# Two attention layers on one core: the single jobs of the first layer placed at other steps, and the softmax denominators' short gaps begun twelve units earlier

## What is computed

```python
px = avg_pool_3x3_s2(x)                         # 28 x 28 keys
q = conv1x1(x, w_qs, b_qs); k = conv1x1(px, w_qs, b_qs); v = conv1x1(px, w_vs, b_vs)
pi = softmax(mix_w @ mean(q))                   # weight of each of two parts of 8 channels
out = sum over parts of pi * softmax(q_part @ k_part / 4) @ v
x = conv1x1(out, w_out) * bn_gamma / sqrt(1 + 1e-5) + bn_beta + x
```

```python
xn = (x - mean_c(x)) / sqrt(var_c(x) + 1e-5) * gamma      # over the 128 channels
q, k, v = split(w_qkv @ xn)                                # 8 heads of 16
h = leaky(w0 @ rel + b0); h = leaky(w1 @ h + b1); bias = w2 @ h + b2   # rel: signed log distances
x = x + w_out @ (softmax(q @ k / 4 + bias) @ v)
```

## Time and profile before

| | |
|---|---|
| median of three executions | 3918.48 us (3915.25, 3918.48, 3929.6) |
| the profiled execution: its time | 3944.19 us |
| its span | 3942.2 us |
| TensorE busy in the span | 3749.5 us, 95%, 27690 matmuls |
| VectorE, ScalarE, POOL busy | 2739.9, 2394.8, 848.9 us |
| mean granted TensorE clock | 0.94 of full |
| first layer, units 0 to 55 | 49.4 to 1390.7 us |
| second layer, units 56 to 83 | 1390.7 us to the end |

### The profile page before, as it was taken

The page is one execution under the profiler, slowest core; times in us unless marked ns, Lnnn a source line. Parts: engine busy times, 40 slices in busy tenths (PEclk is TensorE's granted clock), DMA queues, the critical chain, the costliest instruction groups (busy, mean ns, idle before and its releaser), DMA issues.

```text
span 3942.2 us, 70851 instructions
## 1 busy us (share of the span) xinstructions
PE 3749.5 (95%) x27690; PEld 1043.3 (26%) x27690; DVE 2739.9 (70%) x8284; ACT 2394.8 (61%) x2830; POOL 848.9 (22%) x935
## 2 busy tenths in 40 slices
PE   7998899899887999999999999999999999999998
PEld 2222222222222222222222222222222222222221
DVE  5567777777765777766777666777776677777770
ACT  3556766766766256666566666566666656666665
POOL 2143433434525111122101012101112201000000
PEclk6779998989978699999999999999999999999999
DMA  1288888200002023222223222232232222232320
GB/s 51 17 57 56 58 59 55 27 15 19 18 15 72 22 63 92 70 67 70 68 72 82 70 70 70 70 86 74 70 84 79 71 68 70 67 86 74 82 56 26
DMA packets 268053, 236.35 MB, mean 60 GB/s; under 512 B 222184, under 2 KB 225112, under 8 KB 267464
## 3 DMA queue, kind: packets, MB, share of 16 engines
q1 hardware_dynamic: 241544, 205.85, 27.8%
q0 software_dynamic: 26176, 25.98, 3.1%
HBM read 226.65 MB, written 27.19 MB: 64 GB/s over the span
## 4 chain that ended last, share of the span: by engine, by line
PE 80%; DVE 8%; issue 7%; POOL 2%; ACT 2%; DMA 1%; POOLq 0%; SPq 0%; ACTq 0%; DVEq 0%
PE P L731 25%; PE P L716 18%; PE P L684 15%; PE P L697 7%; DVE maxes L1046 7%; PE P L673 5%; PE P L757 4%; PE P L807 2%; PE P L701 2%; PE P L784 1%; POOL high L539 1%; PE P L773 1%; PE P L819 1%; DVE junk L1065 0%; ACT L984 0%
## 5 line engine op out<-in xcount | busy, mean ns | idle before, releaser
L935 ACT ACTIVATE probs<-P 128x896 f32<-128x896 f32 (+1 forms) x2352 | 2117.2, 916 | 1359.2 <-PE P L716 964.2
L1065 DVE CUSTOM_DVE_ANT_0 junk<-P,mstage 112x448 bf16<-112x448 f32 x3136 | 1773.6, 621 | 675.7 <-PE P L684 675.2
L731 PE MATMUL P<-probs,vals 128*17 128x448 f32 (+1 forms) x9408 | 1181.2, 576 | 11.9 <-ACT sums L1011 11.7
L1046 DVE TENSOR_REDUCE maxes<-P 128x1 f32<-128x392 f32 (+1 forms) x1600 | 796.4, 558 | 338.2 <-PE P L673 337.5
L716 PE MATMUL P<-bstage,flip 112*56 112x448 f16 x6272 | 887.1, 363 | 0.0
L684 PE MATMUL P<-keys,q_stack 48*112 48x448 f16 x3136 | 740.2, 400 | 10.6 <-DVE maxes L1065 9.1
L697 PE MATMUL P<-q_two,keys 49*128 49x448 f16 x3136 | 642.2, 352 | 0.0
L684 PEld LDWEIGHTS P<-keys,q_stack 48*112 48x112 f16 x3136 | 284.7, 124 | 887.9 <-DVE maxes L1065 468.0
L673 PE MATMUL P<-keys,q_stack 24*128 24x392 f16 (+1 forms) x1600 | 416.8, 369 | 84.5 <-DVE maxes L1046 52.7
L539 POOL TENSOR_SCALAR high<-projected,cst 128x448 f16<-128x448 f32 x112 | 157.0, 1402 | 1385.0 <-ACT projected L944 1335.2
L716 PEld LDWEIGHTS P<-bstage,flip 112*56 112x56 f16 x6272 | 210.6, 104 | 572.8 <-issue 572.8
(11 more groups left out here) (129 smaller groups left out, 1444.6 us busy)
## 6 DMA issues: line engine op xcount, KB each, us to landing
mstage<-g_max SPq DMA_DIRECT2D x56, 1519.0 KB, 8.0
bstage<-g_bias SPq DMA_DIRECT2D x28, 1568.0 KB, 8.1
bstage<-g_bias SPq DMA_DIRECT2D x28, 1519.0 KB, 7.9
g_max<-t_bf SPq DMA_DIRECT2D x16, 673.8 KB
keys<-d_rden POOLq DMA_DIRECT2D x42, 224.0 KB, 6.0
rwide<-d_rden POOLq DMA_DIRECT2D x42, 224.0 KB, 4.9
g_bias<-t_hi SPq DMA_DIRECT2D x8, 679.9 KB
g_bias<-t_lo SPq DMA_DIRECT2D x8, 679.9 KB
```

The lines of the kernel that those rows point to most:

```text
L731: last = mm(P[32 * h:32 * h + HD + 1, PV, 0:QB], table[0:kr, kt, h, :], probs[0:kr, s % 3, h, :], start=kt == 0, stop=kt == unit.tiles - 1 ...
L935: A(probs[0:kr, s % 3, 2 * p:2 * p + 2, :], P[0:kr, 2 * p:2 * p + 2, 0:QB], ACT.Exp).then_inc(exp_done, 1)
L1046: V.tensor_reduce(out=maxes0[0:size, unit.i % 2, t, HALVES[r], c:c + 1], in_=P[0:size, bank_of(job), 0:HALF], op=ALU.max, axis=AX.X).then_ ...
L1065: V.tensor_tensor_reduce(out=junk[:, PLAN.nth[job] % 4, :], in0=P[0:QT, bank_of(job), 0:QB], in1=bias, scale=1.0, scalar=-3.0e38, op0=ALU. ...
```

## The change

- `SLOW` goes from 42 to 30. With it the gaps of `stages` shrink from unit 24 on instead of 36 and are two steps from unit 28 instead of 40; units 30 to 41 use `sums` and `rwide`; and `keys[0]` is cleared at steps 223 to 230 instead of 307 to 314.
- The 21 network jobs go from steps 0 to 20 (one in each) to steps 2, 3 and 5 of each of units 0 to 6; the last is at step 47.
- The seven pairs `m`, `w` of the first batch go from steps 350 to 363 (units 50 and 51, one job in each step) to the third and fourth step of units 34 to 40, one pair in each unit.
- The 14 key and 4 value jobs of group 8 go from steps 364 to 381 (one in each) to steps 315 to 367, one in about every third step.
- The value job of groups 1 to 7 goes from four steps behind the first key job to nine behind it.
- Group 8's weights are loaded at step 305 and scaled at 312. Groups 6 and 7 still need their biases then, so there are four buffers of biases, chosen by `biases_of`.

No instruction of arithmetic is added or taken away.

```diff
--- before.py
+++ after.py
@@ -49,7 +49,7 @@
 
 
 
-SLOW, SUMS0, RDEN = 42, 6, 4
+SLOW, SUMS0, RDEN = 30, 6, 4
 CLEARS = 7
 GROUPS0, GROUPS1 = 4, 2
 FIRST1 = NB * GROUPS0 * ROWS8
@@ -168,7 +168,7 @@
                 put(BASE[i] - 1, "b", "s", i, 0)
             put(STAGES[i]["projected"], "b", "o", i)
         for n in range(len(NET)):
-            put(n, "b", "n", n)
+            put(7 * (n // 3) + (2, 3, 5)[n % 3], "b", "n", n)
         put(2, "b", "x", 0)
         put(4, "b", "x", 1)
         for group in range(1, len(UNITS) // ROWS8):
@@ -177,9 +177,11 @@
                 at = BASE[first.i - 3]
                 put(at, "b", "k", group, 0, 0)
                 put(at + 2, "b", "k", group, 1, 0)
-                put(at + 4, "b", "v", group, 0)
+                put(at + 9, "b", "v", group, 0)
                 continue
             before = range(BASE[first.i - 4], BASE[first.i - 2] + UNITS[first.i - 2].tiles - 3)
+            if first.i == FIRST1:
+                before = range(BASE[FIRST1 - 11], BASE[FIRST1 - 3])
             todo = [("k", group, n, p) for n in range(7) for p in range(2)] + [("v", group, m) for m in range(4)]
             for k, job in enumerate(todo):
                 put(before[k * len(before) // len(todo)], "b", *job)
@@ -187,7 +189,8 @@
             first = FIRST1 + b * GROUPS1 * ROWS8
             steps = range(BASE[first - 6], BASE[first - 4])
             for n in range(7):
-                at = steps[2 * n * len(steps) // 14]
+
+                at = steps[2 * n * len(steps) // 14] if b else BASE[FIRST1 // NB + 6 + n] + 2
                 put(at, "b", "m", b, n)
                 put(at + 1, "b", "w", b, n)
 
@@ -237,7 +240,7 @@
         bar = sb("bar", [128, BW])
         pi = sb("pi", [128, 8])
         wg = [sb(f"wg{k}", [128, WG]) for k in range(2)]
-        biases = [sb(f"biases{k}", [128, AW]) for k in range(2)]
+        biases = [sb(f"biases{k}", [128, AW]) for k in range(4)]
         quarter = [sb(f"quarter{k}", [128, 3]) for k in range(2)]
         marks = sb("marks", [128, 4])
         keys = [sb(f"keys{k}", [128, 2, 28 * 128], F16) for k in range(2)]
@@ -335,6 +338,9 @@
         q_flat = q_stack[:, :, :].rearrange("k a n -> k (a n)")
         mean = cst[:, C_MEAN:C_MEAN + 128]
         IDLE0 = PLAN.last("qk", lambda j: j[1] < (FIRST1 if j[0] == "q" else NB * GROUPS0))
+
+        def biases_of(group):
+            return group % 2 + 2 * is_biased(group)
 
         def landed(j):
             return 16 * (j // 2 + 1)
@@ -485,6 +491,7 @@
                     blocks = wg[k][:, QW:QW + 512].rearrange("c (s j) -> c s j", j=64)
                     G.tensor_scalar(narrow[k][:, 0, :, 0:24], blocks[:, 0:4, 0:24], 1.0, None, ALU.mult)
                     G.tensor_scalar(narrow[k][:, 1, :, 0:24], blocks[:, 4:8, 0:24], HD ** -0.5, None, ALU.mult)
+                k = biases_of(group)
                 G.tensor_scalar(biases[k][:, A_Q:A_Q + n], qb, 1.0, None, ALU.mult)
                 G.tensor_scalar(biases[k][:, A_K:A_K + n], kb, HD ** -0.5, one, ALU.mult, ALU.add).then_inc(wg_ready, 1)
 
@@ -604,13 +611,16 @@
                 if s == BASE[8]:
                     pool_source(1)
                 for group in range(2, len(UNITS) // ROWS8):
-                    early_load = group < NB * GROUPS0
+                    early_load = group <= NB * GROUPS0
                     at = BASE[(group - 1) * ROWS8] + 4 if early_load else STAGES[(group - 1) * ROWS8 - 1]["projected"] + 1
+                    if group == NB * GROUPS0:
+                        at = BASE[(group - 2) * ROWS8 + 1] + 4
                     if s == at:
                         if early_load:
 
 
-                            pool.wait_ge(copied, PLAN.last("qk", lambda j: group_of(j) == group - 2))
+                            if not is_biased(group):
+                                pool.wait_ge(copied, PLAN.last("qk", lambda j: group_of(j) == group - 2))
                             pool.wait_ge(vals_made, PLAN.last("v", lambda j: j[1] == group - 2))
                             pool.wait_ge(wg_ready, group - 1)
                             pool.wait_ge(wout_ready, group - 1)
@@ -619,7 +629,7 @@
                         load_group(pool, group)
                     if s == at + 7:
                         scale_weights(group)
-                    if early_load and s == BASE[group * ROWS8] + 10:
+                    if not is_biased(group) and s == BASE[group * ROWS8] + 10:
                         weigh_output(group)
 
         @block.tensor
@@ -936,7 +946,7 @@
 
             def take_projection(job):
                 _, p, width = stack_source(job)
-                k, n = group_of(job) % 2, PLAN.nth[job]
+                k, n = biases_of(group_of(job)), PLAN.nth[job]
                 at = (A_Q, A_K)["qk".index(job[0])] + p
                 act.wait_ge(proj_made, n + 1)
                 if n >= 2:
```

## The result

The changed kernel takes 3980.0 us (median of four runs, 3971.4 to 3997.2) against 3922.3 (median of four, 3915.3 to 3929.6): ratio 1.0153, 95% interval 1.0111 to 1.0195. It is slower by 1.5%, with an interval clear of 1, and outside the forecast range of 3889 to 3948. An execution over 1.5% above the fastest of its kernel is left out of every mean, median and ratio here. The profiled execution is the slowest of the four, with a span of 3995.2 us; the one of the kernel before, with 3942.2, was also dearer than that kernel's median, so the two profiles do not stand for the medians in every stretch.

What follows compares the result with a forecast made beforehand. First-layer units were taken as paced by steps of 2.14 us, extra jobs at 1.2 us and TensorE's half clock. Terms 22 + 2 + 6 + 2 - 33 = -1 gave 3919 us against the median, no change; range 3889 to 3948.

Steps and rivals of the forecast that it cites:

- SLOW 30: Units 28 to 33: short denominator transfers stall while the table is spread; loss 33 us, bounds 10 and 50.
- short legs that don't bite: Rival 1: back-to-back denominator transfers land fast or the spread ends before unit 30; loss at most 5, 3891 us, chance 0.26.
- My ring in POOL's order: Units 28 to 33: product, next load, store back, broadcast, product wait on each other; a 29.8 us turn against 20.2 a unit.
- Keys, values and value jobs: Group 8's jobs out of units 52 to 54, gain 6 us; other groups' value jobs five steps later, gain 2.
- The network: Units 0 to 6: jobs over seven units raise TensorE's granted clock to 0.80; gain 22 us, bounds nothing and 40.
- nothing, if the share stays: Lower bound of the network's gain in units 0 to 6: no gain if the granted clock share does not change.
- The moments: Pairs moved to units 34 to 40: 4.0 us a pair stays of 4.4; gain 2 us, bounds -5 and 14.
- seven pauses, each of which may drop the clock: Lower bound of the moments' term over units 34 to 40: -5 us.
- Rival 2: The ring bites and units 0 to 6 keep their clock: loss 45, gains 15, 3948 us; chance 0.24.
- what would show it: Signs named beforehand: times of units 0 to 6, 28 to 33, 34 to 40, 50 to 55, the spread and the second layer.

Runs made afterwards that it cites:

- e1: The whole change but with SLOW 42 as in the kernel before; median 3944.4 us, ratio to the kernel before 1.0077.
- e13: The changed kernel with POOL's load of the next denominators moved ahead of the product of the unit before; median 3978.0 us, ratio to the kernel before 1.0159.
- e7: The kernel before with only the change's keys, values, value jobs and biases, and the moment pairs packed over units 43 and 44; median 3901.1 us, ratio 0.9923.
- e17: The same kernel as e7, run again in another group; median 3903.4 us, ratio to the kernel before 0.9971.
- e8: e7 with the network dealt over units 0 to 6 as in the change; median 3915.4 us, ratio to the kernel before 0.9988.
- e4: The kernel before with only the first batch's moments moved, one pair a unit over units 34 to 40; median 3927.0 us, ratio 1.0036.
- e9: e4 with three extra 128x448 matmuls on constants in the step behind each w job; median 3920.5 us, ratio to the kernel before 0.9996.
- e14: The changed kernel with three extra 128x448 matmuls in the step behind each first-batch w job; median 3970.2 us, ratio to the kernel before 1.0137.
- e12: e7 with the output projection of units 40 to 55 one step earlier and POOL's clearing of keys[0] begun a step later; ratio to the kernel before 1.001.
- e18: The same kernel as e12, run again in another group; ratio to the kernel before 0.9996.
- e2: The whole change, but the seven first-batch moment pairs one job a step over units 39 and 40; median 3974.1 us, ratio to the kernel before 1.0105.
- e10: The kernel before with one extra 64-column matmul in each first-layer step that has a first-pass group; median 4162.6 us, ratio 1.0576.
- e5: The kernel before with SLOW 30 alone; mean span 3950.9 us, ratio 1.0078.
- e15: The same kernel as e5, run again in another group; mean span 3933.5 us, ratio to the kernel before 1.0045.

## Why the prediction was wrong

**SLOW 30: right that short legs stall beside the spread, and close in size.** The step was a loss of 33 with a turn of 29.8 us and a spread that ends 116 us into unit 28. Measured: legs of 24.0 us in sum for 26.0, turns of 28.2, 25.7 and 22.6, a spread that ends near 815 us, 123 us into unit 28, and, by e1 against the change, a loss of 32 to 36. I had 28 for stalls and 5 for POOL and the clock; the split says 22 and 14, and some 7 of the 14 were stalls at the half clock, so the make-up was about right too. Units 29 to 33 of the profiles: 148.4 us at 0.73 against 103.0 at 0.94 is 148.4 x 0.27 x 2/3 = 27 lost to the clock against 4, and 23 of waits. The chance I gave to short legs that don't bite (0.26) is answered by the two rows of waits. My ring in POOL's order, however, is not shown: e13 opened it at one edge and nothing changed.

By the Trainium skill ("DMA: Bandwidth & Descriptors", the part on the two cost components) a turn would have been some 6.5 us plus handovers, an estimate from its fixed and per-byte cost. Beside the spread this trace does not agree: the three legs alone took 24.0 us.

**Keys, values and value jobs: right in sign, the gain larger.** The terms were 6 and 2, and 2 for the moments as packed as before. Before to e7 and e17 gained 25 and 16 us, of which only 5 are waits and work. Units 52 to 54 fell by 20.5 us, to 77 where 70 was forecast, since their jobs went elsewhere; the wait of ScalarE on POOL's stacks, 7.5 us before, is gone, and that on the denominator load, 6.2 us, which I left standing, is 1.1 us. The rest of the gain is clock, which I did not size and which no run explains.

**The network: the first step that failed.** "I take a granted 0.80" for units 0 to 6 rested on the thought that single jobs raise the clock, so more units with jobs have more rises. In the two profiles the clock there went from 0.66 to 0.70 and the stretch stayed at 217 us; over all profiles the new order has 0.68 to 0.72, and the old one 0.74 to 0.83 wherever but in the one that I read. So the term was wrong in sign, and it started from one execution that was no typical one. The whole-kernel price of the spread network is 3 to 5 us of waits and the rest clock: +8 alone, some +19 on e7. A gain of 22 was a loss of 8 to 19. Why the old order holds the clock better is not shown. The bound "nothing, if the share stays" was too kind as well.

**The moments: the second.** The price of a pair was right: 4.0 was forecast, and waits and work are the same packed or dealt out (e8 and e1, 3784.1 both). What failed was the term's use of "seven pauses, each of which may drop the clock" as a bound of 5 us. Dealt out, the pairs cost 27 us of clock (e8 to e1), 18 in e4, and the fills of e9 and e14 give 27 and 21 to 25 back. A packed run of pairs has its seven pauses in 14 steps, and those steps were at 0.92 in e7; dealt out, 30 of 35 pairs were followed by a stretch at the half clock, 3 to 31 us long, as from 936 to 953 us in unit 36. Rival 2 had both conditions that came true, a ring that bites and a network that gives nothing back, and stalls that drop TensorE to the half clock. It gave 3948, with too small a price, no loss from the network and nothing for the moments.

**The sum.** In place of 22 + 2 + 6 + 2 - 33 = -1 the ladder has -19 - 27 + 20 - 36 = -62, the 20 being the mean of 25 and 16 for all of the first step. Waits and work alone were forecast as gains of some 10 against stalls of 28, so 18 us slower; they are 22 slower. That these are so close is partly luck: the gains in waits were 5 for 10, the network added 5 that I did not have, and the stalls were 22 for 28. What was far off is the clock, which I had as a gain of 22, less a few us within the 5 for POOL and the clock, and which is a loss of 37.

**Of what would show it:** tables stored at 265 us, not 235, since the network's last job comes later than forecast; the last spread transfer landed near 815, not 780, for the same reason; units 28 to 33 at 167 us, not 155; units 34 to 40 at +59, not +28; 50 and 51 at 41, not 37; 52 to 54 at 77, not 70, with 1.1 us of the wait that was to stay at 6; unit 55 at 73 and the second layer at 2553, as forecast.

## What stays open

Which leg of the four makes the stalls, since the one edge that e13 took away only passed the waiting on. Why the network in steps 0 to 20 keeps a higher clock through units 0 to 6 than over seven units. Whether a wide fill elsewhere than behind a pair would help as much. Why e7 loses 12 to 20 us less to the clock than before, and why one step's move of the output projection (e12, e18) gives that back. And whether e7 with the fill of e9 behind its pairs would gain more: it was not tried.

## What to carry to other kernels

Before short-gap orders are moved to an earlier place, see what the DMA queues carry there: the same legs that cost nothing in quiet queues set the pace beside a stream of small packets, and whatever delays that stream's start lengthens the overlap. Work that makes TensorE pause was cheaper here in one place than dealt out, where most pairs were followed by a stretch at the half clock of their own; other matmuls put behind each of them took most of that back. Split every measured span into time lost to the clock and the rest before judging a change, since here the rest repeats to some 2 us and the span to 12 or more. And before a term is built on one profile's stretch, see how that stretch stands in another execution: 49 us of waste in units 0 to 6 were read, where 21 to 35 was usual.

## What the hardware showed that I had not expected

- A busy TensorE kept the half clock: 53 us behind a stall in the changed kernel with TensorE busy 53.1, unit 34 of the kernel before, and units 34 to 38 of e2's dearest execution, 136.7 us with 135.8 busy. The matmuls of these plain steps did not bring it back.
- 21 added matmuls, 12.5 us of work, took 27 us off the clock's loss (e4 to e9), and 21 to 25 in e14; a small one in every step (e10) made the loss 95 us larger instead.
- The clock's loss of one kernel in two groups of some ten executions differed by 18 us (e5, e15), with waits and work the same to 0.2 us.
